# Attention and a routed FFN on one core: the first values piece a step earlier, the maxima's transposition behind it, their placement issued by SyncE

## What is computed

```
scores  = einsum('bhqd,bhkd->bhqk', Q, K) * scale        # 16 heads, 512 x 512, causal
weights = softmax(where(mask, -1e6, scores))
attn    = einsum('bhqk,bhkd->bhqd', weights, V).reshape(b, s, 128) @ Wo + bo
x       = layernorm(x + attn)
x       = layernorm(x + experts(x))                       # top 2 of 8, gelu
```

## Time and profile before

| | before |
|---|---|
| median of three runs | 985.86 us |
| the profiled execution | 977.47 us, its span 975.7 us |
| attention, about 35 to 645 us | TensorE busy 545 of 610 us |
| placements (L335) | 64, issued by ScalarE, 0.61 us each on its queue |
| experts and the last normalisation, about 645 to 975 us | TensorE busy 286 of 330 us |

### The profile page before, as it was taken

One profiled execution on the slowest core, in us unless ns is written; L12 is line 12 of the kernel. 1 busy time (PEld: TensorE's weight loads), 2 busy tenths in 40 slices (PEclk: granted clock), 3 DMA queues, 4 the chain that ended last, 5 costly groups with the idle time before them and its releaser, 6 DMA issues.

```text
span 975.7 us, 28904 instructions
## 1 busy us (share of the span) xinstructions
PE 851.0 (87%) x9151; PEld 561.4 (58%) x9151; DVE 734.4 (75%) x2003; ACT 681.5 (70%) x1451; POOL 662.7 (68%) x911
## 2 busy tenths in 40 slices
PE   5688898988998999989989988779999999999950
PEld 2344354444444444444544544358999988989950
DVE  2887879888988888888899888964554565377756
ACT  2377687777787787777878877755666555668775
POOL 6243555778778778787787786658777656567654
PEclk9799999999999999999999999999999999999985
DMA  7625635636446455345345332253233223365644
GB/s 196 203 75 162 177 89 164 182 106 206 139 135 208 111 165 187 102 145 174 105 161 172 101 126 73 63 143 92 80 89 88 84 78 88 112 212 184 187 133 125
DMA packets 168787, 132.37 MB, mean 136 GB/s; under 512 B 52861, under 2 KB 154532, under 8 KB 168512
## 3 DMA queue, kind: packets, MB, share of 16 engines
q1 hardware_dynamic: 156352, 112.34, 38.8%
q0 software_dynamic: 8640, 17.06, 5.1%
q10 hardware_dynamic: 3648, 1.12, 0.5%
HBM read 71.42 MB, written 61.01 MB: 136 GB/s over the span
## 4 chain that ended last, share of the span: by engine, by line
PE 50%; POOL 17%; issue 11%; ACT 11%; DVE 6%; DMA 4%; SPq 0%; ACTq 0%; POOLq 0%; DVEq 0%
PE ring L1301 12%; PE ring L1285 12%; PE ps_v L1219 6%; PE ring L1156 4%; ACT probs L827 4%; POOL probs L683 4%; PE ring L1187 3%; POOL rows_d L725 3%; POOL rs L749 3%; DVE negmax L1345 2%; PE ps_m L1049 2%; PE ps_m L1055 2%; PE ps_m L1033 2%; PE ps_m L1044 2%; POOL qarea L647 1%
## 5 line engine op out<-in xcount | busy, mean ns | idle before, releaser
L1345 DVE TENSOR_REDUCE negmax<-ring 128x2 f32<-128x1024 f32 (+3 forms) x512 | 407.1, 813 | 62.5 <-PE ring L1202 61.3
L827 ACT ACTIVATE probs<-ring 128x768 f32<-128x768 f32 (+1 forms) x384 | 334.7, 879 | 109.2 <-PE ring L1156 104.9
L683 POOL TENSOR_SCALAR_AFFINE_SELECT probs<-probs 128x512 f32<-128x512 f32 x256 | 162.5, 638 | 149.4 <-ACT probs L827 147.4
L952 ACT ACTIVATE vpad<-ring,b_s 128x128 f32<-128x128 f32 x568 | 162.3, 368 | 105.4 <-PE ring L1285 102.4
L733 POOL DMA_INDIRECT y_d<-vpad,xs x142 | 148.1, 1043 | 81.5 <-DVE vpad L1660 52.0
L1219 PE MATMUL ps_v<-probs,vpad 128*32 128x512 f32 (+3 forms) x2048 | 182.0, 444 | 10.0 <-POOL probs L683 9.8
L1301 PE MATMUL ring<-qarea,vpad 128*128 x1136 | 153.8, 279 | 4.8 <-issue 2.7
L1285 PE MATMUL ring<-kside,w_t 128*128 128x128 f32 x1136 | 152.6, 277 | 1.1 <-issue 0.9
L725 POOL DMA_INDIRECT rows_d<-xn,slot x128 | 129.1, 1008 | 30.2 <-issue 26.3
L1301 PEld LDWEIGHTS ring<-qarea,vpad 128*128 128x128 f32 x1136 | 137.9, 192 | 10.0 <-issue 8.3
L1285 PEld LDWEIGHTS ring<-kside,w_t 128*128 128x128 f32 x1136 | 138.1, 192 | 3.9 <-issue 2.8
(11 more groups left out here) (201 smaller groups left out, 1178.4 us busy)
## 6 DMA issues: line engine op xcount, KB each, us to landing
kside<-qk_d SPq DMA_DIRECT2D x32, 512.0 KB, 4.8
qk_d<-qarea SPq DMA_DIRECT2D x32, 384.0 KB, 2.7
xs<-rows_d SPq DMA_DIRECT2D x142, 66.0 KB
qk_d<-qarea SPq DMA_DIRECT2D x32, 256.0 KB, 2.5
qarea<-qk_d SPq DMA_DIRECT2D x16, 512.0 KB
qodd<-qk_d SPq DMA_DIRECT2D x16, 512.0 KB
probs<-y_d SPq DMA_DIRECT2D x16, 512.0 KB, 5.1
xin<-L_attn_x SPq DMA_DIRECT2D x16, 256.0 KB, 3.5
```

Source lines behind the costliest of these rows:

```text
L683: pool.affine_select(out=diag, in_=diag, pattern=[[0, 4], [1, P]], compare_op=ALU.is_ge, fill=0.0, base=0, channel_multiplier=-1).then_inc ...
L827: nc.scalar.activation(of_unit(h // 2, part), ring[:, 2 * part % 3, :, (0, P, P)[part]:S], ACT.Exp, scale=SCALE).then_inc(sem("exp_done"), 1)
L952: ins = nc.scalar.activation(ht[:, n % 4, c, :], ps_a[:, n % 4, c * P:(c + 1) * P], ACT.Gelu_apprx_tanh, bias=b1_s[:, bass.ds(e, 1), c:c + ...
L1345: ins = nc.vector.tensor_reduce(negmax[:, n // 6 % 2, qb, s:s + 2], ring[:, (2 * n + 1) % 3, :, c0:c0 + nk], AX.X, ALU.max, negate=True)
```

## The change

Three edits, in one:

1. TensorE takes the first values piece (0,) of a group at the end of the step with `h % 4 == 0`, a step earlier. Its wait for the masks asks for one mask less (`- (kbs[-1] < 2)`): pieces (0,) and (1,) read no block that the group's last mask writes; the last piece, which does, has the whole wait now.
2. The product "mT" opens the step with `h % 4 == 1`, ahead of its scores and maxima. ScalarE copies it in the first third of the step, ahead of that step's normalisation and exponential.
3. SyncE issues the placement, between its other transfers, and no longer ScalarE.

```diff
@@ SyncE
             if nxt.exists(NB):
                 need(sp, sem("scores_ready"), UNITS, i, 0, sem("sp_passed"))
                 for k in range(2):
                     for what in (1, 0):
                         place_side(sp, nxt, what, k)
+            place_max(sp, i, 1)
             store_parts(sp, ahead, 1)
+            place_max(sp, i, 2)
...
             elif i.value < NB:
                 store_attention(sp, prev)
+                place_max(sp, i, 3)
                 load_attention(sp, prev)
                 store_x2(sp, prev.plus(-1))
             store_parts(sp, ahead, 0)
+            place_max(sp, nxt, 0)
...
             store_parts(sp, At(1, 1, False), 0)
+            place_max(sp, first, 0)
             load_x(sp, first)
@@ ScalarE
                         if h == 5 and u == 0 and nxt.exists(NB):
                             copy_v(act, nxt)
+                        if u == 0 and h % 4 == 1:
+                            copy_max(act, *((i, 1), (i, 2), (i, 3), (nxt, 0))[h // 4])
...
-                        if u == 2 and h % 4 == 1:
-                            copy_max(act, *((i, 1), (i, 2), (i, 3), (nxt, 0))[h // 4])
                         if u == 1:
                             middle(act, h, i, nxt, prev, rb)
-                            if h % 4 == 2:
-                                place_max(act, *((i, 1), (i, 2), (i, 3), (nxt, 0))[h // 4])
@@ TensorE
+                need(pe, sem("masked"), NH, b, GH * (g + 1) - (kbs[-1] < 2))
                 if kbs[0] == 0:
-                    need(pe, sem("masked"), NH, b, GH * (g + 1))
...
+                    if h % 4 == 1:
+                        misc(i, *MISC[h])
                     scores(i, h // 2, 2 if h % 2 else 0)
                     maxima(mb, mu + (2 if h % 2 else 0), i, h)
-                    if h in MISC:
+                    if h in MISC and h % 4 != 1:
                         misc(i, *MISC[h])
...
-                    if h % 4:
+                    if h % 4 != 1:
                         vb, vg = (i, h // 4 - 1) if h >= 4 else (i.plus(-1), 3)
-                        values(vb, vg, ((0,), (1,), (3, 2))[h % 4 - 1])
+                        values(vb, vg, ((0,), None, (1,), (3, 2))[h % 4])
```

More of the change, by code:

```diff
@@ L328, in along, with place_max @@
             return t.unsqueeze(len(t.shape)).broadcast_to([*t.shape, n])
[L330 removed]
+        def place_max(sp, b, g):
             if not b.exists(NB):
                 return
[L334 to L335 removed]
+            need(sp, freed("mT"), 4, b, g + 1, sem("sp_passed"))
+            sp.dma_start(qside[b.parity][SPARE:P:MSTEP, 2 * g:2 * g + 2, :].rearrange("y e n -> y (e n)"),
                           mt[:, :]).then_inc(sem("max_placed"), 16)
```

3 lines of the change are left out of this document (removed).

## The result

The changed kernel took 1007.0 us (median of 4 runs, 1005.4 to 1009.2) and the kernel before 984.5 (4 runs, 982.2 to 987.9): a ratio of 1.0219, 95% interval 1.018 to 1.0258. It is slower by 22 us. The two profiled executions are 1005.9 and 977.5 us, with spans of 1004.1 and 975.7. The span grew by 28.3 us: 27.3 of it are between the first and the last scores of the attention stage, 1.3 ahead of the first scores, and the part behind the last scores is as long as before (335.5 against 335.8 us).

What follows compares the result with a forecast made beforehand. The prediction took tightly coupled engines, with ScalarE's order setting the pace in steps 5 and 6, as the bound. Reordering +28 us and placements about 0 made 977.5 us 1005.5 profiled and the 985.9 us median 1014, range 992 to 1027.

Steps and rivals of the forecast that it cites:

- Step 5: Attention stage, edits 1 and 2: ScalarE waits for "mT", next exponential 0.62 us late, TensorE 0.6 us late: +0.6 an iteration.
- Step 9: Attention stage, edits 1 and 2: later "mT", copy and exponential delay the next maxima 0.76 us; taken as +0.6 an iteration.
- Step 13: Attention stage, edits 1 and 2, no normalisation there: next maxima 0.77 us late, VectorE's too; taken as +0.7 an iteration.
- Step 1: Attention stage: ScalarE's normalisation waits for GpSimd until 381.16 anyway, so TensorE's saved 0.94 us are spent again: 0.
- Steps 6 to 8: Attention stage: no added loss was forecast there, 0; only that there is no gap in which to catch up.
- Edit 3: Placements issued by SyncE: later landings +2 and the very first placement -1.8 us, about 0 in sum, from -7 to +8.
- The first placement: Ahead of the first scores: it took 4.04 us and would stand ahead of x and the sides: -1.8, between 0 and -2.8.
- The sum: Whole kernel: 28 us for edits 1 and 2, about 0 for the placements, profiled 1005.5, median 1014 us.
- full price of the queue: Rival: losses as forecast, and each first placement also waits for the sides, +10 us more: 1024 us; chance 0.07.
- the filled hole: Rival: the values piece covers TensorE's waits and nothing replaces them, 24 us gained, 6 for placements: 956 us; chance 0.10.
- Absorbed in part: Rival: ScalarE is idle 8 of 38 us, so later parts may absorb loss, +5 to +14: 995 us; chance 0.15.

Runs made afterwards that it cites:

- mask_only: Kernel before with only the values pieces' wait relaxed by one mask, at their old place: 1042.8 us, ratio 0.9972 to the kernel before in its own set of runs.
- after_gamma_later: Changed kernel with GpSimd's product of x with gamma one step later (step 6 in place of 5): 999.5 us, ratio 1.0147 to the kernel before.
- order_only: Changed kernel with the placement issued by ScalarE as before, so edits 1 and 2 alone: 1004.8 us, ratio 1.0198 to the kernel before.
- after: The changed kernel with all three edits, against the kernel before: 1007.0 us, ratio 1.0219.
- before_again: The kernel before, unchanged, run and profiled again under another name: 1044.9 us, ratio 0.9986 to the kernel before in its own set of runs.
- norm_later: mask_only with ScalarE's first two normalisation pieces of x in step 3 in place of step 1: 1032.3 us, ratio 0.9862 to the kernel before.
- norm_later_x2: norm_later with the normalisation pieces of x2 also moved, from step 9 to step 7: 1028.3 us, ratio 0.9843 to the kernel before.
- the four groups: Sets of runs, each on one chip with its own runs of the kernel before, which took 984.9, 1046.3, 1046.5 and 983.6 us.

## Why the prediction was right, and where it was not

The prediction was 1014 us, 992 to 1027, with 0.81 on slower; 1007.0 was measured.

- **Step 5, +0.6.** Measured +0.63. Each link held: "mT" 0.05 us behind the copy of V, the idle time 0.48 (forecast 0.49), the next exponential 0.63 us late (0.62), the maxima of step 6 stand 5.73 us behind the first scores of step 4 where they stood 4.98 (409.29 - 403.56 against 392.85 - 387.87), +0.75 as worked out.
- **Step 9, +0.6.** Measured +0.60. Inside it two sizes were off and cancelled. The maxima of step 10 come 3.69 us behind the second maxima of step 8 in place of 2.76 (418.85 - 415.16 against the earlier trace rows), +0.93 and not +0.76, since "mT" still waits 0.17 us for the copy of the attention: the forecast's 0.08 us between the end of that copy and "mT" was too thin a margin. More was won back behind the maxima than the 0.1 us that was allowed.
- **Step 13, +0.7.** Measured +0.83, the most undersized of the three. Its sum starts the values at 409.8, where its own rule for step 9 (the second maxima's start and 0.39 us) would give 409.96. The maxima of step 14 are as late as worked out (2.96 in place of 2.23 us behind the second maxima of step 12, +0.73 for a forecast of +0.77). Behind them TensorE now waits 0.18 us for VectorE in step 14, where it did not. The forecast named VectorE's part and then rounded down.
- **Step 1, 0.** Measured -0.28, and the step of the reasoning that failed is "which now waits for GpSimd until 381.16 anyway". The copy of the maxima came ahead of that wait, and TensorE, not GpSimd, is what ScalarE waits for there (0.98 us). The forecast's own times say so: a copy that starts at 381.25 and holds ScalarE for 0.47 us ends behind 381.16. The conclusion, that the 0.94 us of TensorE's waits are not won, held: mask_only gave 0.1, edits 1 and 2 together 0.28.
- **Steps 6 to 8, nothing.** Measured +0.53. The forecast followed three engines and left out that VectorE, half a microsecond later against GpSimd, would meet its product with gamma. after_gamma_later shows the term by itself.
- **Edit 3, about 0.** Right in sum (order_only and after differ by 0.2%, inside both intervals), with one term wrong. The first placement took 1.92 us (issued at 35.81, landed at 37.73) in place of 4.04, as hoped, but the first scores start at 39.12 us in place of 37.80, since "mT" at the head of the step waits for VectorE there and holds the maxima behind it:

```profile
34.57 0.59 PE L1066 MATMUL ps_m<-identb,mhl 128*16 128x128 bf16 x4 [3.49 <-DVE mhl L1371]
...
39.12 0.61 PE L1160 MATMUL ring<-qarea,kside 64*128 64x512 bf16 x2 [1.26 <-DVE negmax L1351]
```

  The first scores of the experiments start anywhere from 37.2 to 42.2 us, so the 1.3 us say little either way; the forecast of -1.8 is not borne out. The rule of the Trainium skill that the prediction weighed (page "DMA: Bandwidth & Descriptors", section "Issuing engines are not separate DMA queues") would have had a gain of 6 us here; none came.
- **The sum.** 28 were forecast for the orders and 27.3 came, of them 24.6 in batches 2 to 13: 2.05 each, since the first of them are not yet settled, and 2.8 in batches 0, 1, 14 and 15, for which 5.4 had been allowed. For the profiled execution 1005.5 us was forecast and 1005.9 measured. That this meets to 0.4 us is partly luck: for batches 2 to 13 the orders were forecast at 22.8 us and cost 24.6, with 0.53 us missed and 0.28 unforeseen in each, and the edges gave back what that was short of. The 7 us by which 1014 is above the median come from the last line of the sum: I added 8.4 us, by which the profiled execution of the kernel before was below its median. That distance was a property of that one run: at 977.5 us it is faster than every one of the 30 timed runs of the same kernel that have a median of 984 to 985 us (the fastest took 980.6). The changed kernel's profiled run is 1.1 us below its median. Against the timed runs the change costs 22 us, against the two profiles 28. Iterations with the collision in the timed runs of the kernel before would make such a difference; no run shows it, as the timed ones have no trace here.
- **The rivals.** The full price of the queue and the filled hole didn't happen. "Absorbed in part" was wrong as a mechanism too: next to nothing that was lost by step 6 came back by step 16 (0.05 us, the table's last stretch). Its reasoning, that ScalarE is idle for 8 of 38 us, says nothing on whether that idle time lies behind the loss or in front of it.

## What to carry to other kernels

- In a loop whose engines wait for each other every few hundred nanoseconds, an instruction that only fills another's wait is also what gives that other engine its time. Before it is moved, ask who works during it, and who will be waited for when it is gone. The price was 0.6 to 0.8 us at each of three places, worked out from one copy, one lag of 0.05 us and the order alone.
- The largest term that the prediction missed came from a pair of engines that the edit doesn't touch. When an edit shifts one engine against another by half a microsecond, look for pairs that now overlap, here a short VectorE instruction with two inputs in SBUF beside a long one of GpSimd.
- Predict against the span of the profiled run that the rows come from. Its distance from the median is a fact about that run until several profiles show it.
- Before profiles of two groups of runs are compared, look for a place where they differ that no edit touches. Here it was the exponential of step 4.

## What the runs showed of the hardware that I had not expected

- The same program runs with iterations of two lengths. Before: 37.8 us in one profile, 38.8 in before_again. norm_later shows both within one execution: batches 4 to 8 take 38.7 to 38.8 us, from batch 9 on it is 37.5. In batch 8 VectorE's product starts 0.54 us behind GpSimd's start and takes 0.76; from batch 9 it starts ahead of it and takes 0.21 to 0.40:

```profile
362.73 0.76 DVE L1432 TENSOR_TENSOR gates<-terms,gates 128x4 f32<-128x4 f32 x1
...
438.30 0.23 DVE L1432 TENSOR_TENSOR gates<-terms,gates 128x4 f32<-128x4 f32 x1
```

```profile
362.19 1.28 POOL L764 TENSOR_TENSOR xc<-xc,gam_b 128x512 f32<-128x512 f32 x1
...
438.47 1.28 POOL L764 TENSOR_TENSOR xc<-xc,gam_b 128x512 f32<-128x512 f32 x1
```

  The collision makes VectorE late, and a late VectorE can meet the next one, so it may keep itself up. The traces bear this out only in part. after_gamma_later shows that undoing it pays in the changed kernel. But in its first profile the kernel before collides in batches 3 and 4 and is free of it from batch 5 on, and norm_later_x2, from batch 6 on, collides in batch 10 alone (38.75 us, the batches beside it 37.8 and 37.5). And it is not the only cause: half of before_again's longer iteration is the late exponential of step 4, and in batches 4 to 7 of norm_later TensorE waits 1.3 to 1.7 us for the placement at step 4. No run of the kernel before without the collision separates them.
- In two of the four groups the kernels took about 60 us more. The profiled span of before_again is 67.5 us longer than that of the kernel before: 12 of them are its longer iterations, 2.4 the later first scores; the other 53 are the stage behind the last scores, 388 us against 336, at a mean granted clock of 0.97 over the span in both. In a stretch of 100 us at full clock TensorE is busy for 87.5 us there, and 97.0 in the kernel before's first profile:

```profile
800.00:900.00 100.00, 87.50 (x722) 81.49 (x722) 48.24 (x182) 46.74 (x166) 50.39 (x52) 1.00 0.24 69
```

```profile
800.00:900.00 100.00, 96.99 (x819) 92.95 (x818) 60.04 (x247) 65.37 (x239) 63.45 (x59) 1.00 0.48 150
```

  What holds it back there stays open. The record's chip number does not tell these groups apart: groups 1, 3 and 4 have the same one, group 2 another. In the seven profiles of the two groups that stage takes 384 to 391 us, so it enlarges the denominator of every ratio and adds a scatter of some us. The late exponential of step 4 is in the same profiles and reaches into the attention stage, which the change is about.
- The placement, 16 KB issued on SyncE's queue behind the 2 MB of the sides, lands 5 to 7 us after its issue in batches 1 to 9 of the changed kernel, and 1.8 to 2.0 us after it where nothing is ahead, by the landing events in the trace. The pair 79.27 and 85.50 above shows one. Being issued sooner gained little: in batches 4 to 9 it is issued 3.8 us behind the iteration's start and lands at 8.9 to 10.0; issued by ScalarE at 6.2 to 6.3 in the kernel before, it landed at 9.3 to 11.0.
